# Regrouping the one-hot folds of a four-layer graph network, moving run masks to PSUM, and reordering the norm steps of its third pass

## The reference

```python
# layer 0: per-edge 16x16 matrix from a two-layer net on the edge attributes
messages = einsum('ei,eio->eo', x[src], (relu(attr @ W1 + b1) @ W2 + b2).reshape(-1, 16, 16))
# layer 1: two graph convolutions (width 16 each as staged here)
out = segment_sum(xw[src] * (dis[src] * edge_weight * dis[dst])[:, None], dst)
# layer 2: one 16x16 matrix and one offset per relation (230), hyperbolic maps
m   = einsum('ei,eio->eo', h[src], rel_weight[type230]) + rel_emb[type230]
n   = sqrt(max(sum(m*m), 1e-10)); msg = tanh(0.1*n) * m / (0.1*n)
lam = 2 / (1 - 0.01*sum(msg*msg) + 1e-6)          # weights of the aggregation
# layer 3: one 16x16 matrix per relation (90), times a scalar per edge
msg = einsum('ei,eio->eo', h[src], W_rel[type90]) * e
```

## Time and profile before

| | |
|---|---|
| time, median of 3 runs | 22407.31 us (22362.9 to 22407.92) |
| span of the profiled execution | 16080.2 us |
| a time of its own for that execution | none beside the span |
| mean granted TensorE clock | 0.848 |
| busy in the span | TensorE 77%, VectorE 79%, ScalarE 50%, GpSimd 74% |
| first gather of pass 0, 1, 2, 3, 4 at | 49.5, 4182.6, 6610.9, 9040.0, 12674.8 us |

### The profile page before, as it was taken

The page is one execution under the profiler, slowest core; times in us unless marked ns, Lnnn a source line. Parts: engine busy times, 40 slices in busy tenths (PEclk is TensorE's granted clock), DMA queues, the critical chain, the costliest instruction groups (busy, mean ns, idle before and its releaser), DMA issues.

```text
span 16080.2 us, 197886 instructions
## 1 busy us (share of the span) xinstructions
PE 12414.4 (77%) x62964; PEld 11204.4 (70%) x62964; DVE 12672.3 (79%) x13275; ACT 8008.6 (50%) x6941; POOL 11959.0 (74%) x12266
## 2 busy tenths in 40 slices
PE   6777777777599999599999488888888377777774
PEld 5555555555599998599999377777777376766764
DVE  7777777777577777477777589899989599999996
ACT  1111111111466666466666377777777255555552
POOL 6777777777777777677777677777777577777776
PEclk8888888888799999799999688898888577777776
DMA  1111111111122221122221122222222222222221
GB/s 37 28 27 27 28 28 27 28 28 26 33 40 39 40 39 37 28 40 39 40 39 38 37 48 50 50 51 50 50 47 48 44 61 62 63 60 63 61 62 37
DMA packets 811074, 675.53 MB, mean 42 GB/s; under 512 B 420924, under 2 KB 729500, under 8 KB 810500
## 3 DMA queue, kind: packets, MB, share of 16 engines
q1 hardware_dynamic: 419012, 545.90, 11.4%
q0 software_dynamic: 392000, 128.94, 9.3%
HBM read 507.78 MB, written 166.09 MB: 42 GB/s over the span
## 4 chain that ended last, share of the span: by engine, by line
POOL 57%; issue 20%; DVE 8%; DVEq 8%; PE 6%; DMA 1%; ACT 0%; POOLq 0%; SPq 0%; ACTq 0%
POOL deep L637 54%; DVE big L1292 6%; PE PS L855 5%; DVEq L1040 4%; DVEq L1297 3%; POOL deep L646 3%; DVE sml L1561 0%; DVEq L1232 0%; DVE acc L1229 0%; DMA wgt<-in_edge_weight 0%; DVEq L1286 0%; DVE sml L1553 0%; DVE acc L1566 0%; DVE sml L1554 0%; DVE sml L1558 0%
## 5 line engine op out<-in xcount | busy, mean ns | idle before, releaser
L637 POOL DMA_INDIRECT deep<-table,idx x11750 | 11475.0, 977 | 3824.8 <-issue 3579.0
L797 PE MATMUL PS<-tparts,hot 125*128 125x400 f32 x22000 | 4163.7, 350 | 482.7 <-DVE big L1451 305.4
L797 PEld LDWEIGHTS PS<-tparts,hot 125*128 125x128 f32 x22000 | 4078.7, 192 | 567.4 <-DVE big L1451 387.1
L1292 DVE TENSOR_TENSOR big<-PS,deep 128x768 f32<-128x768 f32 (+4 forms) x2750 | 2984.7, 1085 | 1082.2 <-DMA deep<-table,idx 515.5
L855 PE MATMUL PS<-tparts,rhot 125*128 125x426 f32 (+1 forms) x9000 | 2302.2, 428 | 527.7 <-DVE big L1292 293.8
L855 PEld LDWEIGHTS PS<-tparts,rhot 125*128 125x128 f32 x9000 | 2177.8, 246 | 616.3 <-DVE big L1292 320.7
L944 ACT ACTIVATE hot<-deep,ones_col 128x1536 fp32r<-128x1536 bf16 x1000 | 1447.6, 1472 | 1464.7 <-PE PS L797 1424.8
L754 PE MATMUL PS<-w0b_sb,big 128*128 128x256 f32 x6250 | 1826.1, 437 | 428.4 <-DVE big L1292 390.1
L754 PEld LDWEIGHTS PS<-w0b_sb,big 128*128 128x128 f32 x6250 | 1342.2, 222 | 933.7 <-DVE big L1292 475.0
L869 PE MATMUL PS<-wx,hot 115*128 115x272 f32 x12500 | 1726.1, 293 | 311.1 <-DVE big L1292 311.1
L1275 DVE TENSOR_REDUCE acc<-big 128x64 f32<-128x1024 f32 (+2 forms) x1875 | 1940.6, 1035 | 18.3
(11 more groups left out here) (281 smaller groups left out, 9713.7 us busy)
## 6 DMA issues: line engine op xcount, KB each, us to landing
wide<-edge_types SPq DMA_DIRECT2D x250, 800.0 KB, 6.1
deep<-table,idx POOLq DMA_INDIRECT x11750, 2.4
wide<-pick_codes SPq DMA_DIRECT2D x250, 352.0 KB, 3.5
running<-msg SPq DMA_DIRECT2D x250, 212.5 KB, 2.1
running<-msg SPq DMA_DIRECT2D x250, 200.0 KB, 2.0
running<-msg SPq DMA_DIRECT2D x125, 400.0 KB, 2.5
wide<-in_edge_attr SPq DMA_DIRECT2D x125, 200.0 KB, 2.5
tabo<-pick_codes SPq DMA_DIRECT2D x125, 160.0 KB, 4.6
```

Of the source, the lines that this page charges most:

```text
L637: pool.indirect_dma_start(g[:, j, 0:GW[l]], None, tab_dram[l][:, :], bass.IndirectOffsetOnAxis(ap=idx[:, s, j:j + 1], axis=0)).then_inc(ga ...
L797: last = pe.matmul(o, poneh[0:NQ, m, c], tparts[0:NQ, k, m * JC:m * JC + JC], start=m == 0 and k == 0, stop=m == BK - 1 and k == 1)
L1292: dve.tensor_tensor(products(j), matv(l, j, n), xs, ALU.mult).then_inc(mats_free, 1)
```

## The change

Picks go to 12, 12, 5 and 6 columns in passes 1 to 4, so that 13, 13, 20 and 19 columns are gathered. The table is cut anew per pass: 4 banks of 25 nodes in passes 1 and 2, 5 of 20 in pass 3, 6 of 17 in pass 4. A fold of one column is then 8, 10 or 12 matmuls, of 400, 320 or 290 columns. Passes 3 and 4 get their own codes, turned once between passes 0 and 1. Pass 3 folds its picks in groups of 3 and 2 and its relations in eight groups of 3 and 4 columns (`THREES`); pass 4 folds its picks in three groups of 2. The run masks of passes 3 and 4 and, for four of five slots, of passes 1 and 2 lie in PSUM, where the weights, the node numbers of the mask within a bank and a factor are put as well. In passes 1 and 2 ScalarE copies the running sums. In pass 3 ScalarE squares the messages; the sum and the lower bound come in groups 0 and 1 of the next chunk, and `norms` comes at the end of `one_hots`.

```diff
+    THREES = [(0, 3), (3, 4), (7, 3), (10, 4), (14, 3), (17, 4), (21, 3), (24, 1)]
-    PK = [0, 11, 11, 4, 5]
+    PK = [0, 12, 12, 5, 6]
-    BK, JR = 4, NJ // 4
+    BK = [0, 4, 4, 5, 6]
+    JR = [0, 25, 25, 20, 17]
-    GRP = [(0, 3), (3, 3), (6, 3), (9, 2)]
-    RGRP = [[], [], [], [(0, 4)], [(0, 3), (3, 2)]]
+    GRP = [(0, 3), (3, 3), (6, 3), (9, 3)]
+    RGRP = [[], [], [], [(0, 3), (3, 2)], [(0, 2), (2, 2), (4, 2)]]
+    HALVES_OF = [None, None, None, [(0, 14), (14, CH - 14)], HALF]
+             [(4, 3), (0, 2)] + [(4, 3) if i % 2 == 0 else (0, 4) for i in range(7)] + [(3, 1)],
+             [(2 * (i % 3), 2) for i in range(9)] + [(6, 1)]]
...
+        MASK_BANK = [[None] * 5, [3, 7, 3, 7, None], [3, 7, 3, 7, None], [7] * 5, [7] * 5]
...
@@ ScalarE, passes 1 and 2 @@
+            def pick_chunk(l, it, s, peeled):
...
+                for i, (t0, n) in enumerate(GRP):
+                    if i == 2:
+                        if s >= 2:
+                            running_out(l, it, s - 2)
+                        elif not peeled:
+                            running_out(l, it - 1, s + S - 2)
+                        run_mask(l, it, s)
...
@@ ScalarE, pass 3: one_hots @@
+            def squares(l, it, s):
+                act.wait_ge(messages, it * S + (s + 1))
+                act.activation(sq3, msgv(s, l)[:, :, 0:C], ACT.Square).then_inc(squared, 1)
...
+                for b, (t0, n) in enumerate(HALVES_OF[l]):
                     if b == 1 and l == 3:
...
-                        if s or not peeled:
-                            norms(it * S + s)
+                        if s:
+                            run_mask(3, it, s - 1)
...
+                        if s:
+                            squares(3, it, s - 1)
...
                     act.activation(oneh[:, 0:halves, c], dist[:, 0:halves, c], ACT.Relu,
                                    bias=ones_col[:, 0:1], scale=-1.0).then_inc(oneh_ready, 1)
+                if l == 3 and (s or not peeled):
+                    norms(it * S + s)
...
-                run_mask(l, it, s)
+                if l == 4:
+                    run_mask(l, it, s)
@@ VectorE, pass 3: finish, hyper_chunk @@
-                if j == 2:
+                if j == 0:
+                    dve.wait_ge(squared, it * S + (s + 1))
+                    dve.tensor_reduce(sml[:, 0, :], sq3, AXX, ALU.add)
+                if j == 1:
+                    dve.tensor_scalar(sml[:, 1, :], sml[:, 0, :], MIN_NORM, None, ALU.max).then_inc(norm2, 1)
+                if j == 3:
                     dve.wait_ge(tanhs, it * S + (s + 1))
...
-                    then(dve.tensor_tensor(sml[:, 5, :], sml[:, 4, :], sml[:, 4, :], ALU.mult))
-                    dve.scalar_tensor_tensor(sml[:, 5, :], sml[:, 5, :], -CURV, sml[:, 0, :], ALU.mult, ALU.mult)
+                    dve.scalar_tensor_tensor(sml[:, 5, :], sml[:, 3, :], -1.0, sml[:, 3, :], ALU.mult, ALU.mult)
...
-                then(dve.tensor_tensor(sq, mv, mv, ALU.mult))
-                then(dve.tensor_reduce(sml[:, 0, :], sq, AXX, ALU.add))
-                dve.tensor_scalar(sml[:, 1, :], sml[:, 0, :], MIN_NORM, None, ALU.max).then_inc(norm2, 1)
+                dve.sem_inc(messages, 1)
```

More of the change, by code:

```diff
@@ L120, in build_gnn, with flip_rounds, flip_base @@
     MFREE = 16
-    FLIPS = [1, 3, 4]
-    def flip_rounds(l):
-        cols = NCOL * NCH if l == 1 else TILES
+    CODES = [1, 3, 4]
+    TYPES = [3, 4]
+    TURNS = [("codes", l) for l in CODES] + [("types", l) for l in TYPES]
+    def flip_rounds(y):
+        cols = PK[TURNS[y][1]] * NCH if TURNS[y][0] == "codes" else TILES
         blocks = [(P * b, min(P, cols - P * b)) for b in range((cols + P - 1) // P)]
         return [blocks[r:r + 16] for r in range(0, len(blocks), 16)]
-    def flip_base(l):
-        return sum(len(flip_rounds(k)) for k in FLIPS if k < l)
+    def flip_base(y):
+        return sum(len(flip_rounds(k)) for k in range(y))
     def half_of(l, t):
@@ L531, in _ @@
             for l in range(5):
-                if l in (1, 3, 4):
-                    flip(l)
+                if l == 1:
+                    load_words(src, W_SRC)
+                    for k in CODES:
+                        turn("codes", k)
+                if l in TYPES:
+                    turn("types", l)
                 if l:
@@ L769, in _, with turn @@
             straddle(0)
-            def flip(l):
-                of, one = (flat_h, identh) if l == 1 else (flat_b, identb)
-                pe.wait_ge(flat_ready, FLIPS.index(l) + 1)
-                for r, blocks in enumerate(flip_rounds(l)):
-                    if r:
-                        pe.wait_ge(flip_sb, flip_base(l) + r)
+            def turn(what, l):
+                y = TURNS.index((what, l))
+                of, one = (flat_h, identh) if what == "codes" else (flat_b, identb)
+                pe.wait_ge(flat_ready, y + 1)
+                for r, blocks in enumerate(flip_rounds(y)):
+                    if r or (y and what == "codes"):
+                        pe.wait_ge(flip_sb, flip_base(y) + r)
                     for b, (c0, n) in enumerate(blocks):
@@ L824, in _ @@
             straddle(2)
-            flip(3)
+            turn("types", 3)
             pe.wait_ge(ev["lp_v"], 1)
@@ new lines, in pick_chunk @@
+            def pick_chunk(l, it, s, peeled):
+                y = PICKED.index(l)
+                act.wait_ge(rows_in[s], it * 16 + (row_base(l) + 16))
+                code = rows_h[:, HOME[s], :]
+                for m in range(BK[l]):
+                    last = act.activation(pdist[:, m, :], code[:, 0:NPK * P], ACT.Abs, bias=negbank[:, m:m + 1])
+                last.then_inc(rows_used, 1)
+                act.drain()
+                for i, (t0, n) in enumerate(GRP):
[5 more added lines that the diff above has]
+                        run_mask(l, it, s)
+                    act.wait_ge(picks, it * (S * NGR) + (NGR * (y * NCH + s) + i + 1))
+                    c = slice(t0 * P, t0 * P + n * P)
+                    act.activation(poneh[:, :, c], pdist[:, :, c], ACT.Relu, bias=ones_col[:, 0:1],
+                                   scale=-1.0).then_inc(poneh_ready, 1)
+                act.drain()
@@ L1437, in gcn_pass @@
                 y = PICKED.index(l)
-                then(dve.tensor_copy(iota_jr, iota_f[:, 0:JR]))
+                for s in range(2):
+                    dve.memset(maskv(l, s)[:, :, 0], 0.0)
+                    dve.tensor_copy(iota_jr(l, s), iota_f[:, 0:JR[l]])
+                dve.drain()
+                dve.sem_inc(ev["banks_set"], 1)
                 def pick_sum(s, i):
@@ L1584, in _ @@
                     hyper_chunk(it, s, lambda j, s=s: finish(it - (s == 0), (s - 1) % S, j))
-            for j in range(NQD):
+            for j in range(len(THREES)):
                 finish(IT - 1, S - 1, j)
```

303 lines of the change are left out of this document (179 added, 124 removed).

## The result

The kernel after takes 23,367 us (median of 4 runs, 23,335 to 23,401), the kernel before in the same comparison 22,408: a ratio of 1.0431 (95% interval 1.0413 to 1.045), +959 us. The forecast was slower by 545 us, 22,950, range 22,500 to 23,300. The direction holds; the time lies outside the range, and above the upper end of the forecast's own range too (23,350).

What follows compares the result with a forecast made beforehand. Passes last at least GpSimd's gathers, with TensorE and VectorE close behind or also full. +50 (passes 1 and 2) + 575 (pass 3) - 80 (pass 4) = +545 us: 22,950 us, range 22,500 to 23,300.

Steps and rivals of the forecast that it cites:

- The first step: Whole kernel: terms summed against the profiled 16,080 us span and carried over in microseconds, assuming 6,327 us lie around it.
- the 6,327 us: Whole kernel: median run time of 22,407 us over the profiled span of 16,080 us, assumed to lie around that span.
- Rival (c): Whole kernel: the missing 6,327 us are gathers at 1.80 us each; 500 fewer save 900 us, 21,510 us; chance 0.08.
- Pass 3 (+575): Pass 3: new norm order puts ScalarE's one-hots before the fold; period 27.1 to 31.7 us a chunk, +575 us.
- my account: Pass 3: step times from bound through norms, one-hots, fold and VectorE's picks to the next relation product, 31.7 us.
- T: Pass 3: start of a chunk's first relation product, from which the prediction timed every step.
- the old order's 26.1 us: Pass 3: same sum for the old norm order, 14.8 + 7.6 + 3.7; slower folds were said to give 27 seen.
- a ring of 31 or 27: Pass 3: chunk period set by engines waiting on each other, forecast 31.7 us after against 27.1 before.
- Pass 4 (-80): Pass 4: GpSimd falls to 24.5 us, VectorE leads at 25.1 us a chunk; -80 us.
- Passes 1 and 2 (+50): Passes 1 and 2: the TensorE and VectorE ring takes 18.2 us a chunk, +0.2 a chunk, +50 us for both.
- GpSimd's relief is eaten by TensorE and VectorE: Passes 1 and 2: GpSimd falls to 16.7 us a chunk, but the ring of TensorE and VectorE holds 18.2.
- the gain that I had left as a bound: Passes 1, 2 and 4: scan with mask in PSUM at a product's speed, 0.43 us less each, up to 180 us.

Runs made afterwards that it cites:

- the first profile: Kernel before, unchanged, as profiled for the prediction: span 16,080 us, against a median of 22,407 us in the timed runs.
- few gathers: Kernel after, and kernel before, with most gathers of passes 1 to 4 left out (two a chunk made, other rows stale): 18,361 and 17,561 us.
- The short fold: Kernel after with half of pass 4's fold left out, 36 of 72 matmuls a chunk: 22,562 us.
- the old picks: Kernel after with the old picks (11, 11, 4, 5) and 4 banks in every pass, all else as after: 23,190 us, ratio 1.0341.
- the second profile of before: Kernel before, unchanged, profiled again under the conditions of the timed runs: 22,401 us, span 22,399.6 us.

## Why the prediction was wrong

**The first step failed**: "The sum is made against the span and carried over in microseconds, as if the 6,327 us lay around it." They lie inside, some 14 us a chunk in pass 0 (45.8 against 31.6), 5.6 in passes 1 and 2, 17 in pass 3, 6 in pass 4, and they are starving: 6,697 us of VectorE's waiting were for late signals of TensorE, against none in the first profile. The chunks that I costed don't occur in the timed runs. Rival (c) took the 6,327 us for dearer gathers; they cost 944 to 970 ns there, less than in the earlier trace rows. That the kernel after came out slower, as forecast, is luck: the term that was to make it slower, pass 3, brought 52 of the 959 us.

**Pass 3 (+575): right mechanism, hidden.** The timeline of pass 3 of the kernel after with few gathers follows my account step by step, from T = 12927.97:

```profile
12927.97 1.00 DVE L1396 TENSOR_TENSOR big<-PS,deep 128x816 f32<-128x816 f32 x1
...
12931.80 0.17 DVE L1672 TENSOR_SCALAR sml<-sml 128x25 f32<-128x25 f32 x1
12932.00 0.22 ACT L1067 ACTIVATE sml<-sml 128x25 f32<-128x25 f32 x1 [7.46 <-DVE sml L1672]
...
12933.57 0.22 ACT L1069 ACTIVATE sml<-sml 128x25 f32<-128x25 f32 x1
12933.87 3.71 ACT L1078 ACTIVATE late<-tabo,negbank 128x640 bf16<-128x640 f16 x5
...
12937.48 5.80 ACT L1080 ACTIVATE deep<-wide,negrel 128x3200 bf16<-128x3200 bf16 x2
...
12943.43 2.96 ACT L1084 ACTIVATE hot<-late,ones_col 128x3200 fp32r<-128x3200 bf16 x1
...
12946.52 9.40 PE L914 MATMUL PS<-tparts,hot 125*128 125x320 f32 x50 [4.19 <-DVE big L1396]
...
12958.66 1.00 DVE L1396 TENSOR_TENSOR big<-PS,deep 128x816 f32<-128x816 f32 x1
```

The bound is there at T + 4.0 (I had 4.05), the norms at T + 5.8 (5.9), the one-hots at T + 18.4 (18.75); the fold begins 0.13 us behind them, not behind VectorE, whose products ended at T + 15.7 (16.1), lasts 9.4 us (9.9), and the next T is at 30.7 (31.7). The profile puts TensorE's wait before the fold down to VectorE's product, which had long ended; by the times it is ScalarE's one-hots. From the bound to ScalarE's next work pass 1.9 us, close to the 1.85 that I took from the row and below the 2.66 us by the Trainium skill (ScalarE: Activation LUTs, on what a table load costs). The -1.0 us is fold and VectorE. One support of the account was weaker than I wrote: the old order's 26.1 us already held a slow fold (7.6 us), so slower folds don't lift it to 27; the rows' two folds are 26.75 us apart. In the timed runs both kernels stand at 44 to 45 us a chunk, so a ring of 31 or 27 decides nothing: the pass got 52 us longer. That is the sum's largest term, mis-sized because its cover, the starved TensorE, was not in the profile that I read.

**Pass 4 (-80): wrong sign, +589.** With few gathers the pass comes out near the account (24.5 against 24.9 of before, -54 us). In the timed runs TensorE's instructions in a chunk count. Counted with weight loads and the register and semaphore steps it had some 193 and has 257. A burst of 19 gathers lets through some 150 and then one in 0.70 us, about 190 in all (an estimate from the rows above); before that was just enough. My estimate for the excess of 65, from those numbers: left over until the burst ends, and then followed by the next burst before TensorE has caught up. Every second chunk or so is 40 to 46 us, the others 29.3. The short fold showed that fewer matmuls take the long chunks away, and the old picks took back 336 us; what the other 260 us are is open, as the count was that of before there.

**Passes 1 and 2 (+50): mis-sized, +291.** That "GpSimd's relief is eaten by TensorE and VectorE" held with few gathers (18.1 us a chunk, 18.2 forecast). In the timed runs the new picks even gain there, and the rest of the change costs 1.9 and 1.5 us a chunk for a reason that no run here shows. The scan with a mask in PSUM takes 1.02 us for 416 elements, as the earlier trace rows had it; this agrees with the Trainium skill's rule on feedback (DVE: opcode table, instruction layouts, handler registers and perf-mode slots), and the gain that I had left as a bound was none (0.43 us in 375 chunks would have been 161 us, not 180). A product of 400 elements with its factor in PSUM took 0.94 us, with the factor in SBUF 0.95.

**What stays open**: why the first profile's execution was fed and every later one not, with the same gathers without a break and the same 197,886 recorded instructions; what of passes 1 and 2, and 260 us of pass 4, is left; and what TensorE's instructions or signals share with the gathers. A rival that no run tests is the recording itself: every later time goes with a recorded span within 2 us of it, so no time is known to be of an execution without a record, and what is held up may be the writing of records.

## What to carry to other kernels

If a profile's span and the timed runs differ by a quarter, the profile is not of what is timed: take another before working out any term. A wait of TensorE that is put down to "issue" and moves in equal steps is not noise; look at what another engine does in the same microseconds, here a run of gathers. Where a wait has no releaser ("remote"), compare its end with the end of the work that it needs: that showed signals late by 8 us and more. And a kernel can be made faster by making an engine that fetches ahead wait: one to three pauses a chunk in GpSimd's gathers were worth 14% against the kernel before, and turned a change that lost 4% into one that gains 1.7%.

## What the runs showed of the hardware

- In every execution but the first profile's, while GpSimd issued indirect transfers without a break (one in 1.25 us), TensorE went on at full speed for some 130 to 150 recorded instructions and then started one every 0.70 us, or none, until 1 to 4 us after the last gather had started. With few gathers the 0.70 us steps go, with the same matmuls. In the first profile of the same kernel, with a gather in 1.28 us, there were none.
- In the same stretches TensorE's signals reached VectorE late: 6,697 us of waiting in the second profile of before, none in the first and none in passes 1 to 4 with few gathers.
- It is not the amount of data: the DMA engines' mean busy share was 0.13 over pass 1 of the kernel after, and the first profile of before moved the same 675.53 MB in 16,080 us without it.
- The SBUF page of the Trainium skill (SBUF — State Buffer, Who interferes with whom) says that "DMA never contends with a compute engine." No run here speaks against it for ports; but in these runs gathers do go with a TensorE that is held up.
- TensorE's granted clock was lower where it starved. In pass 1 it was 0.88 in the kernel after and 1.00 with few gathers, as these windows show (stretch, length, TensorE busy with its count, granted clock, DMA share, GB/s), first the kernel after, then the one with few gathers:

```profile
6022.00:9122.00 3100.00, 2564.48 (x11779) 0.88 0.13 29
```

```profile
6020.00:8262.00 2242.00, 2188.98 (x11710) 1.00 0.12 35
```
